# Layer 1's maxima split on VectorE, rounds of 31 and 23 blocks, other moments in the order

## The reference

```python
x = x + _L0_attn_ref(xn, ...) + _L0_ffn_ref(xn, ...)
xn = _layernorm(x, axis=-1)
x = x + _L1_attn_ref(xn, Wq, Wk, Wv) + _L1_ffn_ref(xn, Wg, W1, W2, W3)
```

## Time and profile before

| what | us |
|---|---|
| median of 3 runs (lowest, highest) | 691.94 (689.86, 697.47) |
| the profiled execution | 687.82 |
| its span, first to last instruction | 686.0 |
| TensorE busy | 643.7 |
| VectorE busy | 502.2 |
| ScalarE busy | 450.7 |
| GpSimd busy | 308.7 |

### The profile page before, as it was taken

One profiled execution on the slowest core, in us unless ns is written; L12 is line 12 of the kernel. 1 busy time (PEld: TensorE's weight loads), 2 busy tenths in 40 slices (PEclk: granted clock), 3 DMA queues, 4 the chain that ended last, 5 costly groups with the idle time before them and its releaser, 6 DMA issues.

```text
span 686.0 us, 13133 instructions
## 1 busy us (share of the span) xinstructions
PE 643.7 (94%) x4200; PEld 352.8 (51%) x4200; DVE 502.2 (73%) x1088; ACT 450.7 (66%) x843; POOL 308.7 (45%) x422
## 2 busy tenths in 40 slices
PE   2999987999999999898999999899999999999986
PEld 1876742654544454333466566555656555656221
DVE  3699779787778798777858777876677777666732
ACT  2443258777768878565877676666667667666774
POOL 3256844873155635646482122666365122122550
PEclk9999998999999999799999999899999999999997
DMA  8954216365344434336645444444755554431110
GB/s 232 295 151 146 84 50 184 118 202 158 103 134 135 149 118 127 102 90 197 212 118 175 146 152 132 145 144 141 219 182 164 161 164 134 140 93 37 47 48 16
DMA packets 82965, 95.16 MB, mean 139 GB/s; under 512 B 7249, under 2 KB 70097, under 8 KB 82897
## 3 DMA queue, kind: packets, MB, share of 16 engines
q1 hardware_dynamic: 78800, 85.91, 41.7%
q0 software_dynamic: 4096, 8.40, 4.2%
HBM read 67.68 MB, written 26.21 MB: 137 GB/s over the span
## 4 chain that ended last, share of the span: by engine, by line
PE 75%; DVE 9%; issue 4%; DMA 3%; POOL 3%; ACT 3%; SPq 2%; another core or an unknown queue 1%; POOLq 0%; DVEq 0%; ACTq 0%
PE pv_ps L917 15%; PE slot L888 15%; PE slot L905 13%; PE slot L865 9%; PE slot L878 6%; PE pv_ps L779 5%; DVE mx L1285 3%; PE slot L854 2%; PE slot L925 2%; PE slot L847 2%; DMA wbuf<-in_experts 1%; PE slot L790 1%; PE slot L897 1%; ACT probsT L1047 1%
## 5 line engine op out<-in xcount | busy, mean ns | idle before, releaser
L1285 DVE TENSOR_REDUCE mx<-slot 128x1 f32<-128x512 f32 x512 | 334.9, 685 | 117.7 <-PE slot L888 94.3
L1047 ACT ACTIVATE probsT<-slot 128x512 f32<-128x512 f32 x512 | 284.2, 597 | 90.4 <-PE slot L905 71.7
L888 PE MATMUL slot<-k_stack,q_stack 72*128 72x512 bf16 x512 | 197.9, 387 | 9.6 <-DVE mx L1285 7.9
L905 PE MATMUL slot<-q_stack,k_stack 75*128 75x512 bf16 x512 | 194.6, 390 | 9.4 <-issue 3.6
L917 PE MATMUL pv_ps<-probsT,v 128*32 128x512 f32 x1024 | 140.5, 621 | 0.9 <-ACT probsT L1047 0.8
L1379 POOL TENSOR_TENSOR hid<-th,up 128x512 f32<-128x512 f32 (+2 forms) x56 | 71.2, 1271 | 130.5 <-DVE th L1148 76.6
L888 PEld LDWEIGHTS slot<-k_stack,q_stack 72*128 72x128 bf16 x512 | 50.1, 98 | 131.8 <-issue 74.7
L1367 POOL DMA_INDIRECT yg<-ys_hbm,index x64 | 62.2, 972 | 45.5 <-issue 34.1
L865 PEld LDWEIGHTS slot<-xgT,wbuf 128*128 128x128 f32 (+1 forms) x576 | 75.6, 186 | 12.3 <-issue 1.1
L905 PEld LDWEIGHTS slot<-q_stack,k_stack 75*128 75x128 bf16 x512 | 50.2, 99 | 58.0 <-issue 19.0
L1356 POOL DMA_INDIRECT xs_hbm<-xn,index x64 | 64.0, 1000 | 32.4 <-DVE index L1262 16.4
(11 more groups left out here) (133 smaller groups left out, 605.5 us busy)
## 6 DMA issues: line engine op xcount, KB each, us to landing
wbuf<-in_experts SPq DMA_DIRECT2D x48, 544.0 KB, 4.9
q_stack<-parts_hbm SPq DMA_DIRECT2D x96, 96.0 KB
k_stack<-parts_hbm SPq DMA_DIRECT2D x96, 96.0 KB
wbuf<-in_experts SPq DMA_DIRECT2D x64, 128.0 KB, 2.7
xg<-xs_hbm SPq DMA_DIRECT2D x28, 256.0 KB
ys_hbm<-ys SPq DMA_DIRECT2D x28, 256.0 KB, 2.6
parts_hbm<-parts SPq DMA_DIRECT2D x16, 384.0 KB
xs_hbm<-zeros SPq DMA_DIRECT2D x2, 2048.0 KB, 12.6
```

Of the source, the lines that this page charges most:

```text
L888: nc.tensor.matmul(ps[:, 0:N], q_stack[0:STACK, h, j * P:(j + 1) * P], k_stack[0:STACK, h, :], start=True, stop=True).then_inc(slot_full, 1)
L905: nc.tensor.matmul(ps[:, 0:N], k_stack[0:STACK + MAXROWS, h, j * P:(j + 1) * P], q_stack[:, h, :], start=True, stop=True).then_inc(slot_fu ...
L1047: nc.scalar.activation(probsT[:, k % PROBS, a, :], ps[:, 0:N], ACT.Exp, scale=SCALE).then_inc(slot_free, 1)
L1285: nc.vector.tensor_reduce(mx[:, g, u // J, u % J:u % J + 1], ps[:, 0:N], AXIS.X, ALU.max)\
```

## The change

It has three parts.

First, `MP` of layer 1 goes to VectorE, as four instructions and with a semaphore of its own for each layer; layer 0's stays on GpSimd. Second, `NB` becomes (31, 23). `live(r, q)` is the number of blocks in group q, 4 or, in the last group of a round, 3, and every stage of that group (loads, transposes, matmuls, evacuations, stores) works on that many. 2048 assignments to 16 experts never fill more than 31 blocks of 128, and to 8 experts never more than 23. Third, all the tables of moments are other ones, `EDGE` shifts `M`, `MP`, `NT` and `E`, `PV` of the first and last attention groups, `WARM` goes from 196 to 218, and the planner lets the output of the last sequence but one wait for the last `NT`.

```diff
-NB = (32, 24)
+NB = (31, 23)
...
-SETUP = (2.045, -9.522, 8.07, 1.095, -8.469, -2.988, -1.684, 25.862)
-ROUTE = (0.046, 0.046, 31.138, 28.95)
-WEIGH = 0.485
-GROUPS = ((4.838, 0.586), (17.79, 0.521), (16.756, 0.924), (29.504, 0.606))
-SLACK = 0.253
-LAG = {'RF': (2.324, -1.184), 'M': (-1.1, -0.238), 'MP': (0.506, 0.56), 'NT': (0.625, -0.823), 'E': (1.07, 3.793), 'PV': (0.552, 0.573), 'PO': (4.67, 1.118), 'AT': (23.765, 0.84), 'WL': (-0.359, -0.605), 'XL': (-0.911, 0.582), 'GG': (-0.389, 5.152), 'DN': (0.742, -0.665), 'YS': (0.607, -1.125), 'YG': (-0.253, 1.108), 'RK': (0.014, 2.373), 'SL': (-1.025, 0.721), 'HI': (17.634, 0.832), 'PW': (5.769, -0.579)}
-WARM = 196
+SETUP = (-0.695, 0.841, 18.925, 2.848, -0.743, 0.439, -0.45, 55.043)
+ROUTE = (0.221, -0.267, 39.524, 55.145)
+WEIGH = -0.735
+GROUPS = ((4.099, 0.012), (19.4, 0.15), (22.028, 0.357), (34.395, 21.863))
+SLACK = 0.248
+LAG = {'RF': (29.209, -5.905), 'M': (-8.645, -1.876), 'MP': (10.243, 0.332), 'NT': (-0.311, -0.786), 'E': (2.619, 1.196), 'PV': (0.23, 4.744), 'PO': (23.903, -0.819), 'AT': (38.004, 0.548), 'WL': (0.038, -9.252), 'XL': (7.501, -0.284), 'GG': (5.744, 8.118), 'DN': (0.49, 1.168), 'YS': (-0.383, -0.166), 'YG': (0.413, 0.607), 'RK': (-0.103, 38.272), 'SL': (-6.744, 13.188), 'HI': (16.955, -0.351), 'PW': (29.653, 1.015)}
+WARM = 218
...
+EDGE = {'0.0': (1.045, -0.333), '0.1': (0.614, -0.352), '0.2': (-0.846, -0.908), '0.3': (-0.161, -0.538), '1.0': (1.021, 0.623), '1.1': (-0.896, 0.617), '6.3': (0.665, -1.261), '7.0': (0.167, 0.05), '7.1': (-0.227, 0.366), '7.2': (-1.203, 1.13), '7.3': (4.35, 0.456)}
...
+            m, e = EDGE.get("%d.%d" % (A, g), (0.0, 0.0))
             for u in range(HG * J):
-                put(t + LAG["M"][l] + u / 16, "M", A, g, u)
-            put(t + LAG["MP"][l], "MP", A, g)
-            put(t + LAG["NT"][l], "NT", A, g)
+                put(t + m + LAG["M"][l] + u / 16, "M", A, g, u)
+            put(t + m + LAG["MP"][l], "MP", A, g)
+            put(t + m + LAG["NT"][l], "NT", A, g)
...
+def live(r, q):
+
+    return min(4, NB[r // 2] - 4 * q)
...
+def maxima_by(A):
+
+    return "DVE" if A >= B else "POOL"
...
-            add(pool, ("MP", A, g), 1.7, 1.75, (dve, ("M", A, g, HG * J - 1)), chain="MP")
-            add(pe, ("NT", A, g), 0.25, 0.5, (pool, ("MP", A, g)), chain="NT")
+            by = maxima_by(A)
+            add(by, ("MP", A, g), 1.7 if by == pool else 0.7, 1.75 if by == pool else 0.8, (dve, ("M", A, g, HG * J - 1)),
+                chain="MP")
+            add(pe, ("NT", A, g), 0.25, 0.5, (by, ("MP", A, g)), chain="NT")
...
-            add(pe, ("DN", r, q), (0.92, 2.8)[l], (1.2, 3.1)[l],
+            add(pe, ("DN", r, q), (0.23, 0.7)[l] * live(r, q), (0.3, 0.775)[l] * live(r, q),
...
-                    for b in range(4):
+                    for b in range(live(r, q)):
                         last = nc.tensor.transpose(ps[:, b * P:(b + 1) * P], xg[:, q % 2, b, :], ident[:])
...
+                elif kind == "MP":
+                    A, g = stage[1:]
+                    ve.wait_ge(*emptied(("M", A, g, HG * J - 1)))
+                    hi, mid, lo = (mx_parts[:, g, :, a, :] for a in range(3))
+                    largest = mx[:, g].rearrange("p h j -> p j h")
+                    link(nc.vector.tensor_scalar(hi, largest, -1.0, None, ALU.mult))
+                    nc.vector.scalar_tensor_tensor(out=mx_rest[:], in0=largest, scalar=-1.0, in1=hi,
+                                                   op0=ALU.mult, op1=ALU.subtract)
+                    link(nc.vector.scalar_tensor_tensor(out=mid, in0=largest, scalar=-1.0, in1=hi,
+                                                        op0=ALU.mult, op1=ALU.subtract))
+                    nc.vector.tensor_tensor(lo, mx_rest[:], mid, ALU.subtract).then_inc(mxp_done[A // B], 1)
```

More of the change, by code:

```diff
@@ L131, in moments @@
             t = GROUPS[r][0] + GROUPS[r][1] * q
-            for b in range(4 * q, 4 * q + 4):
+            for b in range(4 * q, 4 * q + live(r, q)):
                 put(t + LAG["WL"][l], "WL", r, b)
@@ L374, in tasks @@
             r, q = rest
-            add(pe, stage, 0.92, 1.2, (act, ("XG", r, q)), (sp, ("WL", r, 4 * q + 3)), chain="gated")
+            add(pe, stage, 0.23 * live(r, q), 0.3 * live(r, q), (act, ("XG", r, q)), (sp, ("WL", r, 4 * q + live(r, q) - 1)), chain="gated")
         else:
@@ L379, in tasks @@
             for part in (stage, up):
-                add(pe, part, 0.92, 1.2, (act, ("XG", r, q)), (sp, ("WL", r, 4 * q + 3)), chain="gated")
+                add(pe, part, 0.23 * live(r, q), 0.3 * live(r, q), (act, ("XG", r, q)), (sp, ("WL", r, 4 * q + live(r, q) - 1)), chain="gated")
         add(act, stage, 0.5 if up else 1.0, 0.66 if up else 1.2, (pe, stage), *free, chain="gated")
@@ L637, in both_layers @@
         v_done = sem("v_done")
-        mxp_done = sem("mxp_done")
+        mxp_done = [sem(f"mxp_done{l}") for l in range(2)]
         mx_in = [sem(f"mx_in{g}") for g in range(G)]
@@ L851, in _ @@
                     pe.wait_ge(*emptied(("XG", r, q)))
-                    pe.wait_ge(w_in[r][q], 64)
-                    for b in range(4):
+                    pe.wait_ge(w_in[r][q], 16 * live(r, q))
+                    for b in range(live(r, q)):
                         last = nc.tensor.matmul(ps[:, b * P:(b + 1) * P], wbuf[0][:, buffer_of(r, 4 * q + b), 0:P],
@@ L1003, in _ @@
                         sc.wait_ge(h_done, n - 1)
-                    nc.scalar.activation(th[0:rows, n % 2, :], ps[0:rows, 0:N], ACT.Tanh, scale=0.5)\
+                    w = N if kind == "SG" else live(*stage[1:3]) * P
+                    nc.scalar.activation(th[0:rows, n % 2, 0:w], ps[0:rows, 0:w], ACT.Tanh, scale=0.5)\
                         .then_inc(th_done, 1)
@@ L1011, in _ @@
                         sc.wait_ge(h_done, n - 1)
-                    nc.scalar.activation(up[0:rows, n % 2, :], ps[0:rows, 0:N], ACT.Copy, scale=0.5)\
+                    w = N if kind == "SU" else live(*stage[1:3]) * P
+                    nc.scalar.activation(up[0:rows, n % 2, 0:w], ps[0:rows, 0:w], ACT.Copy, scale=0.5)\
                         .then_inc(slot_free, 1)
@@ L1147, in _ @@
                     ve.wait_ge(*filled(source))
-                    nc.vector.scalar_tensor_tensor(out=th[0:rows, n % 2, :], in0=th[0:rows, n % 2, :], scalar=1.0,
-                                                   in1=slot[plan.ring[source]][0:rows, 0:N], op0=ALU.add, op1=ALU.mult)\
+                    w = N if source[0] == "SG" else live(*source[1:3]) * P
+                    nc.vector.scalar_tensor_tensor(out=th[0:rows, n % 2, 0:w], in0=th[0:rows, n % 2, 0:w], scalar=1.0,
+                                                   in1=slot[plan.ring[source]][0:rows, 0:w], op0=ALU.add, op1=ALU.mult)\
                         .then_inc(free_of(source), 1)
@@ L1378, in _ @@
                         gp.wait_ge(*filled(plan.down_of(n - HIDS)))
-                    nc.gpsimd.tensor_tensor(hid[0:rows, n % HIDS, :], th[0:rows, n % 2, :], up[0:rows, n % 2, :], ALU.mult)\
+                    w = N if source[0] == "SG" else live(*source[1:3]) * P
+                    nc.gpsimd.tensor_tensor(hid[0:rows, n % HIDS, 0:w], th[0:rows, n % 2, 0:w], up[0:rows, n % 2, 0:w],
+                                            ALU.mult)\
                         .then_inc(h_done, 1)
```

31 lines of the change are left out of this document (17 added, 14 removed).

## The result

The changed kernel takes 705.81 us in the median of four runs (703.10 to 707.13), the kernel before, beside it, 690.90 (687.23 to 697.47). The ratio is 1.020, 95% interval 1.011 to 1.029: slower, with an interval above 1, and outside the forecast's range of 668 to 697. A second measurement gave 1.0248 [1.0205, 1.0292].

What follows compares the result with a forecast made beforehand. TensorE's queue, nearly without holes from 100 to 660 us, was taken as the bound. 687.8 - 5.3 - 0.9 - 5.0 = 676.6 us, 680.7 by the median; own range 672 to 687, wider range 668 to 697.

Steps and rivals of the forecast that it cites:

- The removed blocks: One block fewer per round in TensorE's full stream, layers 0 and 1: all on the path, 5.3 us saved.
- Maxima on VectorE: Layer 1's parts of the maxima move from GpSimd: 0.9 us gained once, at the last group; nothing at the other fifteen.
- Rival C: VectorE's parts of the maxima meet GpSimd's operations; at four of sixteen, +20 us: 702, by the median 706; chance 0.07.
- The other moments: New tables of moments: 5.0 us gained at the start, nothing taken for middle and end.
- The start: Layer 0's maxima come earlier, ahead of setup and routing: bounds -13 and +3 us, middle -5 taken.
- The middle: TensorE's 16 us of idle from 100 to 660 us are the most an order can win; nothing taken.
- The pauses: Waits without a named cause (4.38 us before 87.21) may or may not come again; counted at nothing.
- A: Order gives nothing at the start, or wins there and loses mid-kernel: 681.6, median 685.7; chance 0.22 together with another rival.
- B: Last round sinks into the tail behind attention; at 35 us later 702.9, by the median 707; chance 0.11.
- P: Theory of the experiments, not the forecast: GpSimd's long unbroken runs of indirect DMAs pause the engines; the change lengthens the pauses.

Runs made afterwards that it cites:

- the idle chains: Kernel before, orders kept, 31 and 23 blocks, layer 1's maxima on VectorE, GpSimd keeping the wait and five useless operations in their place: 0.9982, 688.5 us.
- experiment 2: Against the kernel before at 691.1 us: changed kernel again 1.0248, with four indirect DMAs under way 1.0136, only blocks planned anew 1.0071, only maxima planned anew 1.0101.
- experiment 5: Five GpSimd operations behind each pair of layer 1's indirect DMAs: on kernel before with own orders, 31 and 23 blocks 1.0220, on the change 1.0223; before 667.2 us.
- experiment 4: Kernel before (689.9 us), orders kept, maxima moved, 31 and 23 blocks 1.0217; plus useless GpSimd chains 0.9982; plus breaks behind DMA pairs 1.0290; maxima move alone 1.0192.
- the spaced kernel: Kernel before, orders kept, 31 and 23 blocks, layer 1's maxima on VectorE, five useless GpSimd operations behind every pair of indirect DMAs: 1.0290.
- experiments 1 and 5: The first, before at 666.6 us: four indirect DMAs under way on change 1.0102, on before 1.0001; change with old moments 1.0054, with maxima on GpSimd 1.0105.
- the bound of two: Changed kernel with only two of GpSimd's indirect DMAs under way, each pair waiting until the pair before has landed: 1.0270 of the kernel before at 692.3 us.
- a bound that is free there: Changed kernel with only four of GpSimd's indirect DMAs under way: 1.0102; the same bound in the kernel before (666.6 us): 1.0001.

## Why the prediction was wrong, step by step

- **The removed blocks, -5.3 us.** Not resolved: 0.9968 with the orders kept is -2.2 us, interval -6.1 to +1.7, which holds both nothing and -5.3. And it can hold only if the orders stay; planned anew the same removal cost 0.7 per cent.
- **Maxima on VectorE, -0.9 us.** With the orders kept, this is the step that failed most. The working priced the added side well (0.9 us for four instructions; the groups sum to 14.6 us over sixteen, 0.91 each) and saw that fifteen are covered. The removed side was taken as "GpSimd's five instructions go", a pure relief. In truth it moved everything behind them in GpSimd's fixed queue: indirect DMAs that had been 4 + 4 became eight in a row, at two places. That is worth 16 to 18 us at the upper level. How much of it sits in the changed kernel, whose order is a new one, was not measured: the change with the maxima on GpSimd ran at the lower level alone, and costs the same there (1.0105 and 1.0102).
- **Rival C, +20 us.** Its 706 came near the 705.8 by the wrong mechanism, and by a slip too: its 702 leaves the -5.0 out, 676.6 + 20 is 697, by the median 701. Both are luck. Meetings did happen (two of the 64 new instructions took over 1 us, two 0.8), but they were few, and the idle chains give all the time back with the VectorE instructions in place. The rule quoted from the Trainium skill ("SBUF — State Buffer", section "Who interferes with whom") says that a VectorE instruction with two SBUF inputs and a GpSimd one that reads SBUF shut each other out for a whole instruction. The trace agrees at the one two-input instruction that was long (L1317 at 429.70 us, 1.13 for a median of 0.17, between two GpSimd operations of 1.2 us), and it has no say in the 16 us.
- **The other moments, -5.0 us.** The start was read well: -8.1 us at group 3 by the trace, inside -13 to +3 (-1.1 at the lower level). The middle, "I take nothing", is the step that the runs show wrong in the changed kernel itself: 11 us are lost between groups 3 and 7 at both levels, some 5 of them at the late stacks and the clock behind. Alone, the moments are at 1.0139 [1.0051, 1.0228], some +10 us.
- **The pauses, "nothing".** They were in the rows, they had no cause, and they were set to zero because they "may or may not come again". They came twice as often (8 waits of VectorE for 4), and of the 2.0 to 2.5 per cent they are what the lower level doesn't have, 1.0 to 1.5.
- **Rivals A and B.** A had the right picture (wins at the start, loses in the middle), but ended at no change. B didn't happen.

The parts don't add: -0.3, +2.7 and +1.4 per cent would be 3.8 (with an error of about 1.2, an estimate from the two intervals), and the change measures 2.0 to 2.5. In the change the maxima move in an order with other runs of indirect DMAs; whether that is the reason was not shown.

What stays open: what a pause is, and what sets the level. The traces show VectorE and ScalarE starting late on finished matmuls, at once, in the runs of indirect DMAs, at the upper level only; they don't show what holds them up. The level isn't shown to belong to a chip: the record gives the number 11 to the chip of experiment 2 (691.1 us) and to that of experiment 5 (667.2). Nor was it separated whether GpSimd's wait or its five operations make the break, and the maxima's move was not run with kept orders at the lower level, where P says it costs nothing. P as the reason for the 16 us thus rests on experiment 4, the two traces beside it and the count by the length of the runs. The amount of pauses doesn't order the kernels by itself: the spaced kernel and the moments alone have few or none and are among the slowest.

## What to carry to other kernels

Work taken from an idle engine is not free when that engine's queue is in a fixed order: price what moves up behind it, and on GpSimd count how many indirect DMAs then follow each other unbroken. Look at the clock behind a hole on TensorE of about 2 us: at the two places shown here its fall cost as much as the hole or more, at others it didn't fall. And with a planner in between, hold the orders fixed and change one part before believing any sum: a removal of work that is planned anew may cost more than it saves.

## What the runs showed of the hardware that was not expected

- The same kernel has two levels, 666.6 and 667.2 us in experiments 1 and 5 and 689.9 to 692.3 otherwise, 3.6 per cent apart, and the traces differ: at the upper level all but two have waits without a releaser of up to 6.1 us (the bound of two and the spaced kernel have none), at the lower none. A result at one level says little for the other: the change costs 2.0 to 2.5 per cent at the upper and, with a bound that is free there, 1.0 at the lower.
- At the upper level, reductions and exponentials begin 1.0 to 5.2 us late in or just behind unbroken runs of GpSimd's indirect DMAs, 1.25 us apart: in 58 of 70 runs of six or eight, 32 of 121 of four, 0 of 292 of two. Never more than two under way (the bound of two) or in a row (the spaced kernel) left none.
- TensorE's granted clock fell to 0.50 for 6 us behind a hole of 1.86 us, and to 0.50 and 0.72 for 10 us behind one of 2.3 us in the last groups. Behind a hole of 2.07 us at 317 us of the kernel before it stayed at 1.00. By the mean clock over the span the changed kernel gives up at most 24 us (705.2 x 0.034) and the kernel before 18.5 (686.0 x 0.027), an estimate that also counts low stretches in which TensorE had nothing to do.
